# Edge flags of the second graph layer made on ScalarE, and the combining joined to the experts' stage

## The reference, cut to what matters

```
xn = layernorm(x)
x  = x + gnn0(xn, src, dst) + mix0(xn)
x  = x + experts0(layernorm(x))              # top 2 of 8, weighted
xn = layernorm(x)
x  = x + gnn1(xn, src, dst) + mix1(xn)       # gnn1: 8 heads of 32, elu
x  = x + experts1(x)

gnn1:  e   = leaky_relu(a1[src] + a2[dst])                 # per head
       ex  = exp(e - m[dst])                               # m: the largest e of the node
       out[dst] = sum(ft[src] * ex) / sum(ex)
mix1:  k = softmax(k over nodes); out = q @ (k^T v)
       gate = sigmoid(gelu(xn * g + b @ Wg1 + bg1) @ Wg2 + bg2); (out * gate) @ Wproj + bproj
```

## Time and profile before

| | us |
|---|---|
| median of 3 runs (2297.82 to 2306.29) | 2304.07 |
| profiled execution | 2316.74 |
| its span | 2314.7 |
| busy in the span: PE, DVE, ACT, POOL | 1655.3, 1170.6, 646.7, 1009.7 |
| mean granted TensorE clock | 0.851 |

### The profile page before, as it was taken

How to read it: one execution, slowest core, us unless ns; L and a number is a source line. 1 busy time by engine, 2 the same in 40 slices (tenths; PEclk the granted TensorE clock), 3 DMA queues, 4 the chain that set the end, 5 groups by cost and what they waited for, 6 DMA issues and landing times. The chain is left out here.

```text
span 2314.7 us, 34196 instructions
## 1 busy us (share of the span) xinstructions
PE 1655.3 (72%) x9465; PEld 1344.3 (58%) x9465; DVE 1170.6 (51%) x3308; ACT 646.7 (28%) x2160; POOL 1009.7 (44%) x1091
## 2 busy tenths in 40 slices
PE   5176677676877978999364665676677776699991
PEld 4154455465655557999243453555455555589991
DVE  7255666454556564212543565556566667742223
ACT  4122111122312554232141122332222222543320
POOL 4566566555452002555025555545444440325550
PEclk9589889788889989999686877788888888599996
DMA  7333232222221036666433222222222220267676
GB/s 172 89 89 86 75 85 81 80 79 74 72 72 40 1 100 218 210 214 196 120 96 83 81 74 77 72 72 76 68 67 67 69 65 17 67 205 215 211 206 178
DMA packets 147984, 244.23 MB, mean 106 GB/s; under 512 B 53353, under 2 KB 83352, under 8 KB 147542
## 3 DMA queue, kind: packets, MB, share of 16 engines
q0 software_dynamic: 48384, 134.19, 20.8%
q1 hardware_dynamic: 97290, 106.27, 15.6%
q10 hardware_dynamic: 2124, 1.54, 0.3%
HBM read 210.48 MB, written 31.21 MB: 104 GB/s over the span
## 5 line engine op out<-in xcount | busy, mean ns | idle before, releaser
L646 POOL DMA_INDIRECT es_rows<-table,eall x784 | 746.0, 952 | 746.0 <-SPq L635 436.9
L666 PE MATMUL bank<-es_msg,es_one 128*125 128x264 f32 x976 | 308.1, 469 | 98.9 <-DVE es_msg L785 88.7
L729 ACT ACTIVATE es_oneT<-bank 125x512 bf16<-125x512 f32 x244 | 145.3, 595 | 795.3 <-remote 554.9
L666 PE MATMUL bank<-es_rows,es_won 128*125 x976 | 293.0, 451 | 67.3 <-DVE es_won L782 49.1
L666 PEld LDWEIGHTS bank<-es_msg,es_one 128*125 128x125 f32 x976 | 210.4, 227 | 151.1 <-DVE es_msg L785 98.1
L666 PEld LDWEIGHTS bank<-es_rows,es_won 128*125 128x125 f32 x976 | 205.9, 222 | 111.0 <-issue 76.4
L1193 PE MATMUL bank<-ffn_xbT,ffn_w 128*128 128x128 f32 x1792 | 221.4, 277 | 0.0
L685 PE MATMUL bank<-es_ident,es_one 128*125 128x128 bf16 x976 | 111.0, 243 | 148.8 <-ACT es_oneT L729 85.9
L1346 DVE TENSOR_TENSOR ffn_shared<-bank,ffn_b2s 128x256 f32<-128x256 f32 x112 | 47.6, 425 | 331.0 <-issue 167.8
L1242 ACT ACTIVATE ffn_shared<-bank,ffn_b1s 128x128 f32<-128x128 f32 x448 | 128.1, 369 | 301.1 <-PE bank L1193 288.0
L1193 PEld LDWEIGHTS bank<-ffn_xbT,ffn_w 128*128 128x128 f32 x1792 | 212.1, 194 | 0.1
(11 more groups left out here) (422 smaller groups left out, 2369.6 us busy)
## 6 DMA issues: line engine op xcount, KB each, us to landing
ffn_w<-in_L_ffn_W SPq DMA_DIRECT2D x112, 512.0 KB
es_rows<-table,eall POOLq DMA_INDIRECT x784
ffn_w<-in_L_ffn_W SPq DMA_DIRECT2D x2, 4096.0 KB
xrows<-acc SPq DMA_DIRECT2D x10, 560.0 KB
ct_yy<-yrows SPq DMA_DIRECT2D x10, 560.0 KB
ffn_w<-yrows SPq DMA_DIRECT2D x10, 560.0 KB
table<-acc SPq DMA_DIRECT2D x5, 577.5 KB
table<-acc SPq DMA_DIRECT2D x5, 564.4 KB
```

What stands on the lines that cost most here:

```text
L646: pool.indirect_dma_start(rows[:, q % R, w, :], None, m.table[H], bass.IndirectOffsetOnAxis(ap=m.eall[:, at:at + 1], axis=0)).then_inc(gat ...
L666: ins = pe.matmul(sum_banks[p % 2][0:P, 0:W], left, right, start=(w == 0), stop=(w == BW - 1))
L729: a.activation(oneT[:, p % 2, :], turn_bank[0:P, :], ACT.Copy).then_inc(kept, 1)
```

## The change

In the second edge sums (H > 1) the flags are made by ScalarE: four Squares, one for each group of 128 edges, of (end - node), and one Relu over all of 1 - that. Its place is at the end of ScalarE's step i, for step i + 1. In the first edge sums VectorE still makes them, now behind the reduce. In both, ScalarE waits for `landed` and tells VectorE by `ready`; VectorE adds behind the logit and not at the step's start; VectorE's columns are loaded behind the product and without checks, and ScalarE has a block column with checks.

`combine_tables1` becomes a class `Combine`, whose parts are run inside the experts' stage: SP's loads follow the wait for the last scatter, the products of the weights (`fold`) lie in the experts' loop at j = 10 to 18, and the tables follow the loop. The gate's turns and GELUs move to step 0 of the second edge sums' side work. Some buffers of the experts' stage now lie in `m.xT`.

```diff
+                def flag(p):
+                    tile, blk = tile_of(p), block_of(p)
+                    if p >= O:
+                        a.wait_ge(summed, p - O + 1)
+                    if p >= 1:
+                        a.wait_ge(squared, p)
+                    nodes = m.nodes[:, bass.ds(tile * P, P)]
+                    for w in range(BW):
+                        ins = a.activation(one[:, p % O, w, :], nodes, ACT.Square, bias=m.ends[:, bass.ds(blk * BW + w, 1)], scale=-1.0)
+                    ins.then_inc(squared, 1)
+                    a.wait_ge(squared, p + 1)
+                    a.activation(one[:, p % O, :, :], one[:, p % O, :, :], ACT.Relu, bias=1.0, scale=-1.0).then_inc(marked, 1)
+
+                if H > 1:
+                    flag(0)
                 for i in range(STEPS + 4):
...
                     if valid(i):
                         keep(i)
+                    if valid(i - 2):
+                        a.wait_ge(landed, block_of(i - 2) + 1)
+                        a.sem_inc(ready, 1)
+                    if H > 1 and valid(i + 1):
+                        flag(i + 1)
...
                 for i in range(STEPS + 5):
                     p, p3, p5 = i, i - 3, i - 5
-                    if valid(p5):
-                        add(p5)
-                    if valid(p):
-                        mark(p)
                     if valid(p3):
                         v.wait_ge(scored, p3 + 1)
                         v.tensor_reduce(near[:, p3 % 2, :, :], ...).then_inc(zchain, 1)
+                    if H == 1 and valid(p):
+                        mark(p)
                     if valid(p3):
                         here = rows_of(p3, D, D + H)
-                        v.wait_ge(landed, block_of(p3) + 1)
+                        v.wait_ge(ready, p3 + 1)
...
                         v.tensor_scalar(zq, zq, 0.0, None, ALU.min).then_inc(zed, 1)
+                    if valid(p5):
+                        add(p5)
...
                     if valid(p3):
                         weigh(p3)
+                    for of, p, turn in ((tile_of, i + 3, 5), (block_of, i + 2, 6), (slot_of, i - 1, 1)):
+                        if i % LOAD == turn and valid(p):
+                            of(p)
...
                 for s in range(SY):
                     sp.wait_ge(y_out[s], 16 * (NB // SY))
+                if after is not None:
+                    after.sync(sp)
...
+                    if after is not None and j == after.BIAS:
+                        after.biases(pe)
+                if after is not None:
+                    after.tensor(pe)
...
+                    if after is not None:
+                        after.fold(v, j)
+                if after is not None:
+                    after.vector(v)
...
         if i == 0:
             pe.wait_ge(self.zeroed, 1)
             pe.matmul(total[:, :], self.zeros[:, :], blank, start=True, stop=False)
+            pe.wait_ge(self.gated, 1)
+            for g, tiles in enumerate(self.groups):
+                if g >= 2:
+                    pe.wait_ge(self.gate_bent, g - 1)
+                for t in tiles:
+                    at = (t - tiles[0]) * P
+                    ins = pe.transpose(m.bank[4 + 3 * (g % 2)][0:D // 4, at:at + P], m.tail[:, t, HEADS:], m.ident[0:P, 0:P])
+                ins.then_inc(self.zturned, 1)
         if i == 1:
+            pe.wait_ge(self.gate_bent, len(self.groups))
...
+        for g, tiles in enumerate(self.groups if i == 0 else ()):
+            n = len(tiles) * P
+            a.wait_ge(self.zturned, g + 1)
+            a.activation(m.hgT[:, tiles[0] * P:tiles[0] * P + n], m.bank[4 + 3 * (g % 2)][0:D // 4, 0:n], ACT.Gelu,
+                         bias=m.gate_bias[:, 0:1]).then_inc(self.gate_bent, 1)
```

More of the change, by code:

```diff
@@ L618, in of @@
                         m.steps[0:1, kind, lo:lo + n], engines=[eng.engine], min_val=1 if kind == DONE else 0, max_val=top,
-                        skip_runtime_bounds_check_because=None if kind in (BLK, DONE) else "the step table's entries are within these bounds")
+                        skip_runtime_bounds_check_because=None if checked else "the step table's entries are within these bounds")
                     held.update({lo + u: r for u, r in enumerate(regs)})
@@ L971, in _, with experts @@
                 unrolled(body, 8)
-def experts(nc, m, tag, gb, W1, b1, W2, b2, weighted, jobs, out):
+def experts(nc, m, tag, gb, W1, b1, W2, b2, weighted, jobs, out, follow=None):
     C = 5
@@ L1415, in sem @@
             return c.sem("ct1_" + n)
[L1417 to L1425, removed]
+        self.nc, self.m, self.halves, self.jobs_in, self.loads = nc, m, halves, jobs_in, loads
@@ new lines, in __init__ @@
+        self.pr = sb("pr", [128, D])
+        self.half, self.other, self.shifted, self.shift = [sb(n, [P, NT]) for n in ("half", "other", "shifted", "shift")]
+        self.bits = sb("bits", [P, NT], I32)
+        self.xn = room.rearrange("p (s d) -> p s d", d=D)
+        self.yy_in = [sem(f"yy_in{i}") for i in range(2)]
+        (self.first, self.shifted_set, self.used, self.counted, self.chain, self.normed, self.turned, self.staged, self.rowed,
+         self.row_kept, self.stored, self.biased, self.scaled) = [
@@ new lines, in load, with store @@
+        def load(u):
+            for x in range(2):
+                copy_rows(sp, self.halves(u, x), m.yrows[x * N:(x + 1) * N, :].rearrange("(p t) d -> p t d", p=P)[:, u * C:(u + 1) * C, :],
+                          self.yy_in[u % 2])
+        def store(u):
+            sp.wait_ge(self.row_kept, (u + 1) * C)
+            copy_rows(sp, table[:, u * C:(u + 1) * C, :], m.acc[:, u * C:(u + 1) * C, 0:table_width(HEADS)], self.stored)
+        load(0)
+        load(1)
+        for u in range(NT // C):
+            if u + 2 < NT // C:
+                sp.wait_ge(self.used, (u + 1) * C)
+                load(u + 2)
+            if u >= 2:
+                store(u - 2)
@@ new lines, in scalar, with norm @@
+    def scalar(self, a):
+        m, ENDS, W, xn, shift = self.m, self.ENDS, self.W, self.xn, self.shift
+        def norm(t):
+            a.wait_ge(self.shifted_set, sum(t >= end for end in ENDS) + 1)
+            if t >= 4:
+                a.wait_ge(self.turned, t - 3)
+            a.activation(xn[:, t % 4, :], m.xs[:, t, :], ACT.Identity, bias=shift[:, t:t + 1], scale=m.rstd[:, t:t + 1]).then_inc(self.normed, 1)
+        norm(0)
+        for t in range(NT + 2):
+            if t + 1 < NT and t + 1 not in ENDS:
+                norm(t + 1)
+            if t < NT:
+                a.wait_ge(self.turned, t + 1)
+                a.activation(m.xT[:, :, tile_cols(t)], by_feature(m.bank[t % 2]), ACT.Copy).then_inc(self.staged, 1)
+            if t >= 2:
+                row = m.bank[2 + t % 2]
+                a.wait_ge(self.rowed, t - 1)
+                a.activation(m.acc[:, t - 2, 0:D + HEADS], row[0:P, 0:D + HEADS], ACT.Copy)
+                a.activation(m.tail[:, t - 2, :], row[0:P, D + HEADS:W], ACT.Copy).then_inc(self.row_kept, 1)
+            if t + 1 < NT and t + 1 in ENDS:
+                norm(t + 1)
@@ L1862 @@
 class Mix1:
+    GROUP = 4
     KEYS = 2
```

263 lines of the change are left out of this document (118 added, 145 removed).

## The result

The changed kernel takes 2384.66 us (median of 4 runs, 2369.97 to 2396.11), the kernel before beside it 2305.18 (2297.82 to 2309.00): a ratio of 1.036, 95% interval 1.0316 to 1.0404, or +73 to +93 us. The forecast was +74 us, 2378. The profiled execution has a span of 2368.3 us against 2314.7, so it shows 54 us of the 80: the one of the changed kernel was the fastest of its four, the one of the kernel before (2316.74) slower than all the others of that kernel here.

A forecast was written before the change was run, and what follows sets the result against it. A two-step loop in the second edge sums was taken to bind: turn, ScalarE's copy, exponent, product, sums, and late-seen TensorE work during GpSimd's gathers. 79 + 0 + 0 - 12 + 7 = +74 on 2304 gives 2378 us, range 2335 to 2425.

The forecast's parts named there:

- Steps 1 to 3: Second edge sums: flags on ScalarE, VectorE's new order and the landed wait moved to ScalarE together cost +79 us.
- step 4: Register loads in both edge sums: VectorE's savings and ScalarE's added checked loads cancel, 0 us, bounds -82 and +82.
- step 5: First edge sums: the add fills a wait (-20), small operations stand behind remote waits (+22); taken as 0 us.
- two prices: Second edge sums: 1.1 us for each of 44 pairs with remote waits, 1.8 for each of the other 17.
- My last test: Edge sums' loop: refuted if two steps without a GpSimd run take 11.8 us or less at the same granted clock.
- A: Rival: VectorE binds and gets faster, GpSimd's holds may swallow ScalarE's work; -109 us, 2195 us; chance 27%.
- C: Rival: ScalarE becomes the bound in full, its work paid in every pair; +174 us, 2478 us; chance 8%.
- D: Rival: Square or Relu needs two table loads in each step of the second edge sums; +313 us, 2617 us; chance 1%.
- Step 6: Combining: loads go out 8.7 us earlier and the stage ends 3.0 us earlier without its GELUs; -11.7 us.
- The GELUs at the start: Start of second edge sums: moved GELUs spread under GpSimd's first run, delaying the first product; +7 us, bounds 0 and +35.

The follow-up runs named there:

- run 4: Kernel before with only the combining joined to the experts' stage and the gate's turns and GELUs moved to step 0 of the second edge sums: 2289.56 us, ratio 0.9942.
- run 7: Kernel before plus five idle Squares a step on ScalarE in the second edge sums, behind the copy of the turned flags: 2388.73 us, ratio 1.0261.
- run 8: Kernel before plus the same five idle Squares a step on ScalarE, ahead of the copy of the turned flags: 2344.82 us, ratio 1.0058.
- run 1: Changed kernel with ScalarE making the flags of step i+1 ahead of its wait for the turned flags of step i: 2305.28 us, ratio 1.0005.
- Run 11: Kernel before with only the second edge sums' flags moved to ScalarE, behind the copy of the turned flags: 2397.53 us, ratio 1.0401.
- run 3: Changed kernel with the marks (flags) of the second edge sums back on VectorE, behind its reduce: 2279.31 us, ratio 0.99.
- run 12: Changed kernel with ScalarE's two register loads in the second edge sums put ahead of its wait for the turned flags: 2374.89 us, ratio 1.0205.
- run 10: Changed kernel with plain copies by SyncE in place of GpSimd's gathers in the second edge sums: 2189.59 us, ratio 0.9526 to the kernel before.
- run 9: Kernel before with plain copies by SyncE in place of GpSimd's gathers in the second edge sums: 2108.52 us, ratio 0.9141.
- run 5: Changed kernel with the second edge sums' marks back on VectorE and VectorE itself waiting for landed rows: 2291.39 us beside 2329.06, ratio 0.9832.
- run 6: Changed kernel with ScalarE's flags ahead of the copy of the turned flags and VectorE itself waiting for landed rows: 2311.51 us, ratio 0.993.

## Why the prediction was right

**The sum.** +74 forecast, +80 by the medians. Range and sign held, and so did the mechanism, work behind ScalarE's wait that is paid in part. That the number came so close is partly luck: as far as the runs can be subtracted from each other, the flags were priced too high and the register loads at nothing, and the two errors cancel.

**Steps 1 to 3, the second edge sums: +79 forecast.** The stage as a whole, with the loads of step 4 and the GELUs, took 77 us more in the two profiles. The medians say more: +80 for the kernel, 13 won by run 4's part, and by step 5 perhaps 9 to 12 in the first edge sums, which leaves about 102 to 105, as much as the 104 between the two kernels without holds.

The mechanism, that ScalarE's work behind the release is paid and the same work ahead of it nearly not, is shown by runs 7 and 8, where nobody waits for the work (47 us between the places), and by run 1 against the changed kernel. The price is not the one that I gave. Run 11 (92 us) and run 3 (106) hold the flags together with loads; less the 36 us of run 12, and if costs add up, the flags are 56 to 70 us, 0.9 to 1.1 us a pair for my 1.8 and 1.1. Only their length was right: 1.92 us in the timeline, for 1.8. Against this stands what VectorE's new order and loads gave, 25 us, which I had put at nothing.

My reason for two prices, that behind a GpSimd run a later product only delays the next run, is not shown. The profiles give 77 us with holds and 104 without, but two profiles with the old edge sums differ by 21 us (778.9 and, in run 4, 758.2), by the medians no difference is left, and a part of the 104 is clock. That idle work costs 60% of its length a pair (run 7) is no test of it either: it wasn't run without holds.

What I didn't see is that the turn itself waits for the flags (130 us in the trace; the price of it in time is not measured by itself). I followed the flags to the exponent queued behind them, and not to their first reader. So of what the flags cost, the path through the exponents is shown by run 7, and the one through the turn is seen only as a wait.

**My last test was badly put.** I wrote that the loop is not what I say if two steps without a run of gathers still take 11.8 us or less at the same granted clock. From product to product two steps take 10.5 us in run 10 and 8.9 in run 9, at 0.87 and 0.94. The 11.8 us were one pair, with side work in it and at a granted clock of 0.63, as the busy time of that stretch shows (columns as in the earlier trace rows):

```profile
1713.00:1725.00 12.00, 9.13 (x41) 7.09 (x42) 6.60 (x15) 2.59 (x11) 3.44 (x4) 0.63 0.11 27
```

So the condition of the test is not met, and it decides nothing. The two runs beside each other are the better one: without holds the change still costs time, 81 us.

**Rivals.** A: VectorE did get faster (68 us less busy), and the exponents' wait for it fell from 161 to 27 us, but the time went to the wait for ScalarE. That the holds swallow ScalarE's work behind the release is refuted by run 7, which costs 60 us; whether they swallow a part of it is open. C, every pair in full, would have been +174. D did not come: no table load stands at the Squares.

The Trainium skill (ScalarE: Activation LUTs, Rules for kernel authors) would have the relu on VectorE; run 3 against the changed kernel agrees, with 106 us, and so does run 5 against run 6, where the flags have their best place, with one point. By its budget the flags would take 2.3 us; the trace has 1.92 from first start to last end.

**Step 4, the loads: 0 forecast, wrong.** I set VectorE's 41 us of idle time against 41 us on ScalarE and called the sides equal. The block column's load with its checks was well priced (2.6 us in the trace, forecast 2.7), but I missed that the flags bring the tile column's load behind the release too, 0.55 us more. In their place there the two are paid for the most part: 36 us by run 12, 2.4 a time. VectorE's side was worth at most the 25 us of run 5 against run 4, and these hold the new order as well. So the term is about +11 us (36 - 25) or more, inside my bounds of 82.

**Step 5, the first edge sums: 0 forecast, -12.1 in the profiles, and not clear of noise.** Over all the profiles with the old order it took 685.5 to 700.4 us, with the new one 674.3 to 710.7; the means, 693.3 and 684.7, differ by 9 us. The upper end, run 12, has the same first edge sums as the changed kernel's 677.5, so one profile against another says little. All of it is inside my bounds of -50 and +60. The waits that were put down to "remote" lost 34 us there, but the copy's waits for TensorE rose by 40, from 94.3 to 134.0, and VectorE's for ScalarE's word are new:

```profile
ACT es_oneT L730 <- remote: 230.0, 48, 8.9
...
DVE es_z L826 <- ACTq L757: 157.5, 61, 6.1
...
ACT es_oneT L730 <- PE bank L685: 134.0, 59, 7.4
```

**Step 6, the combining: -11.7 forecast,** -11.9 between the barriers in the profiles of the two kernels, -8.7 in run 4's profile, and -13 for run 4 as a whole, with the GELUs moved. The loads go out at 1100.25, with no barrier before them, and the first weighted add is at 1107.51:

```profile
1100.25 0.36 SPq L2208 DMA_DIRECT2D ffn_w<-yrows  x1
...
1107.51 2.07 DVE L1527 SCALAR_TENSOR_TENSOR xs<-ffn_w,cw,xs 125x256 f32<-125x256 f32 x5 [10.04 <-DMA ffn_w<-yrows]
```

**The GELUs at the start: +7 forecast, 0 to +2 measured, and my picture was wrong.** They are not spread over tens of us:

```profile
1184.08 2.60 ACT L2049 ACTIVATE hgT<-bank,w_gate_bias 64x500 f32<-64x500 f32 x4
...
1187.23 0.67 ACT L2049 ACTIVATE hgT<-bank,w_gate_bias 64x500 f32<-64x500 f32 x1 [0.55 <-PE bank L1965]
1188.07 0.93 ACT L2049 ACTIVATE hgT<-bank,w_gate_bias 64x500 f32<-64x500 f32 x2 [0.16 <-issue]
...
1216.30 0.60 ACT L730 ACTIVATE es_oneT<-bank 125x512 bf16<-125x512 f32 x1 [20.17 <-remote]
```

All seven are done in 4.9 us, as in quiet, and the hold comes after them. The first product starts 50.6 us behind the stage's barrier (1220.6 - 1170.0), before 48.5 (1240.9 - 1192.4). In run 4, which has the GELUs there but not the flags, it is 48.5 again, so my lower bound of 0 was the near one.

## What to carry to other kernels

Before moving work to an engine that looks idle, ask what that engine waits for and what stands behind the wait: five instructions and the register loads that came with them cost 82 us more behind ScalarE's wait than ahead of it, though the engine was busy for 46% of the stage. 36 of these are the loads and their checks, which no share of busy time shows; look also for loads that moved work pulls along with it. Follow moved work both to what is queued behind it and to its first reader, and judge a bundle by its parts: here a bundle that lost 3.6% held one part of 4 to 5% and others worth 1.7% the other way. And don't read one stage's gain or loss from two profiles alone: edge sums that differ in seven GELUs alone gave 758 and 779 us.

## What the runs showed of the hardware

**The holds go with GpSimd's gathers.** With the same rows' worth of bytes asked for by SyncE (run 9), the second edge sums took 566 us instead of 779, and no wait of that stage in either plain run is put down to "remote". The semaphore events of the traces give the time from the end of a TensorE instruction to its update. In run 9's stage all 498 came within 0.02 us. In the kernel before, 43% of 497 came over 1 us late; of the 189 for which GpSimd had been issuing in over 70% of the 5 us before, 89% did, and the median of these 189 was 4.4 us. The runs don't tell whether it is GpSimd's issuing or the indirect kind of DMA, as both went together.

**A run has to last before it holds.** At the start of the stage the gathers begin at 1170.70, and for some 20 of them TensorE's turns are still seen at once; the next turn is held for 20 us:

```profile
1170.70 0.99 POOL L646 DMA_INDIRECT es_rows<-table,eall  x1 [71.98 <-POOLq L81]
...
1193.11 0.60 ACT L730 ACTIVATE es_oneT<-bank 125x512 bf16<-125x512 f32 x1 [1.57 <-PE bank L685]
...
1195.57 0.45 PE L685 MATMUL bank<-es_ident,es_one 128*125 128x128 bf16 x4 [2.57 <-issue]
...
1200.82 0.36 DVE L816 TENSOR_REDUCE es_near<-bank 128x64 f32<-128x192 f32 x1 [18.84 <-remote]
```

Why the hold begins only after some 25 us, no run here shows. The GELUs, done by 1189.0, came before it.

**Small activations overlap.** Four Squares of 128x125, 0.39 us each, take 1.26 us together in the median; without the bias from memory, each waiting for the one before (run 7), one takes 0.31 us.
